# Attention sums read back packed by head and divided as rows of features, instead of turned on TensorE, divided and turned back

## The chip, the cores and the metric

One core of a Trainium2 chip runs the kernel. The metric is the device time of one execution in microseconds (us). Engines are named as in the profile: PE is TensorE (PEld its weight loads), DVE is VectorE, ACT is ScalarE, POOL is GpSimd, and SP is the engine that issues most of the DMAs.

## The reference

Two graph layers over N = 4096 nodes with 128 features. The first is masked attention with 8 heads of 16, a projection with a residual, and a feed-forward part; the second is a softmax over neighbours and a last layer norm.

```python
# layer 0
q, k, v = (layer_norm(x, g1, be1) @ w_qkv).reshape(n, 3, 8, 16) parts
scores = jnp.where(adj != 0, einsum('nhd,mhd->hnm', q, k) * SCALE, -inf)
attn = softmax(scores, axis=-1)
out = einsum('hnm,mhd->nhd', attn, v).reshape(n, 128)
x = x + out @ w_proj + b_proj
x = x + gelu(layer_norm(x, g2, be2) @ w1 + b1) @ w2 + b2
# layer 1
h = x @ Wt.T + bt
s = leaky_relu(h @ Wa.T + ba)
w = softmax(where(adj > 0, s, NEG), axis=1)
out = layer_norm_affine(x + (w @ h) @ Wp.T + bp)
```

## The kernel before

The queries are cut into 8 chunks of CH = 512, each of four subtiles of 128. The main loop goes over 512 steps (chunk, key tile of 128, half of the heads). A step makes scores on PE, masks and exponentiates them on DVE, ACT and POOL, and adds `products` to a PSUM bank. A column of ones stands behind each head's values, so each head gives 17 rows: 16 weighted sums and the denominator. The four heads of a half start at partitions 0, 32, 64 and 96. `copy_acc` (L1412) copies the finished rows of a chunk to `acc_sb`, and SP stores them in the DRAM tensor `a_dram` of shape (8, 128, 2, 512).

Then comes the tail, which the change touches, again by chunks `c`. In the kernel before a chunk goes through these steps:

- `load_sums` on SP (L247, L248): one DMA for the sums of a chunk, one for its rows of x, into two buffers by turns. Both count on the semaphore `acc_in`.
- `turn_acc` on PE (L689): eight 128x128 transposes of the sums to query-major form, into two PSUM banks.
- `normalise_att` on DVE (L484, L491): the reciprocal of the denominators, 128x32, and two products of 128x256 into `att`.
- `turn_att` on PE (L698): four transposes back to feature-major; `turned_att` on ACT (L378) copies them to `attT`.
- `project` on PE (L710): `attT` times `w_proj`.
- `first_sum` on DVE (L503 to L515): plus x and bias (`input_bias` on POOL, L318), and the layer norm's statistics; `root` on POOL (L322); `normalise_x1` on DVE (L522).
- `turn_h2` on PE (L718), `turned_h2` on ACT (L384), `ff1` on PE (L736, two instructions of the profile for one matmul of 512 columns) and `gelu` on ACT (L391), four each; `ff2` on PE (L745).
- `second_sum` on DVE (L532), `turn_x2` on PE (L728), `turned_x2` on ACT (L398), `hidden` on PE (L753) and DVE (L540), `hidden_high` (L402) and `hidden_middle` (L407) on ACT, `hidden_parts` (L546, L549) and `hidden_low` (L555) on DVE.

After that the neighbour sums of layer 1 run over all chunks (L803, L814 and others), on edges that SP began to load (`load_edges`, L255) during this stage.

There is no planner: each engine has one program in a fixed order, and semaphores order the engines against one another. An engine waits in place, so all that stands behind a waiting instruction in its program waits too. DVE's order in the tail is

```python
            for i in range(NC):
                if i >= 2:
                    hidden_low(i - 2)
                if i + 1 < NC:
                    first_sum(i + 1)
                    normalise_x1(i + 1)
                second_sum(i)
                if i + 2 < NC:
                    normalise_att(i + 2)
                if i >= 1:
                    hidden(i - 1)
                    hidden_parts(i - 1)
```

The last four steps of `products` of the main loop are woven into the start of PE's tail.

Of the kernel before, what the change touches and what calls it, by code (L numbers as in the profile page):

```python
# [8 lines left out]
ALU = mybir.AluOpType  # L9
ACT = mybir.ActivationFunctionType  # L10
# [3 lines left out]
P = 128  # L14
D = 128
H, HD = 8, 16
HG = H // 2
CH = 512
SUB = CH // P
VW = HD + 1  # L20
RT = 32
# [16 lines left out]
def gnn_kernel(nc, x, adj, adj_t, wq_rows, wk_rows, wv, w_proj, b_proj, w1, b1, w2, b2, g1, be1, g2, be2,  # L38
               Wt, wt_t, bt, Wa, ba, wp2, bp, gamma, beta, out):
    N = x.shape[0]  # L40
    NT, NC = N // P, N // CH
    TLS = 2 * NC * NT
# [5 lines left out]
    a_dram = nc.dram_tensor("attn_t", (NC, P, 2, CH), F32).ap()  # L48
# [3 lines left out]
    with ExitStack() as ctx:  # L52
        def sb(name, shape, dt):
            return ctx.enter_context(nc.sbuf_tensor(name, shape, dt))

        def sem(name):
            return ctx.enter_context(nc.semaphore(name))
# [11 lines left out]
        identf = sb("identf", [P, P], F32)  # L69
# [9 lines left out]
        ps = ctx.enter_context(nc.psum_tensor("ps", [P, 8, CH], F32))  # L79
# [73 lines left out]
        premasked = sem("premasked")  # L153
        opened = sem("opened")
# [8 lines left out]
        eb = taker(adj_words, q_words)  # L163
# [9 lines left out]

        x2_sb = wb(NT, D)
        h3 = wb(NT * 96).bitcast(BF16).rearrange("p (t k) -> p t k", k=3 * HID)
        acc, xr, xb = [eb(2, CH), eb(2, CH)], [eb(SUB, D), eb(SUB, D)], [eb(SUB, D), eb(SUB, D)]
        att, attT, x1 = eb(SUB * H, HD), eb(CH), eb(SUB, D)
        x1b, h2, h2T = eb(SUB, D), eb(SUB, D), eb(CH)
        ff, hsum, onesf = wb(FF // P, CH), eb(SUB, HID), eb(P)
        bn2, mv2, rl, rstd2 = eb(SUB, 6), eb(SUB, 2), eb(2 * SUB * HG), eb(SUB)  # L180
        x2, x2T = wb(SUB, D), wb(CH)
        hid, rest_h = wb(SUB, HID + 1), wb(SUB, HID)
        s_row, e1, e0, mx = wb(NT), wb(NT), wb(NT), wb(NT)
# [4 lines left out]
        den, aw, ew = wb(SUB), wb(SUB), wb(SUB)  # L188
# [6 lines left out]
        B_FF, B_OUT, B_ACC, B_TURN, B_HID, B_PROJ = 0, 2, 3, 5, 6, 7  # L195
# [3 lines left out]
        tail_in = sem("tail_in")  # L199
        acc_in = [sem("acc_in0"), sem("acc_in1")]  # L200
        wa_made, wa_copied, bt_step = sem("wa_made"), sem("wa_copied"), sem("bt_step")
        acc_turned = sem("acc_turned")
        rl_made, att_made = sem("rl_made"), sem("att_made")
        att_turned, attT_made = sem("att_turned"), sem("attT_made")
        projected = sem("projected")
        xb_made = sem("xb_made")
        x1_made, bn2_made, mv2_made = sem("x1_made"), sem("bn2_made"), sem("mv2_made")
# [2 lines left out]
        h2_made, h2_turned, h2T_made = sem("h2_made"), sem("h2_turned"), sem("h2T_made")  # L210
# [29 lines left out]
        def proj_bank(c):  # L240
            return B_PROJ if c > 0 else B_FF + 1

        def load_sums(sp, c):
            if c >= 2:
                sp.wait_ge(acc_turned, c - 1)
                sp.wait_ge(xb_made, c - 1)
            sp.dma_start(acc[c % 2][:, :, :], a_dram[c, :, :, :]).then_inc(acc_in[c % 2], 16)  # L247
            sp.dma_start(xr[c % 2][:, :, :], x[c * CH:(c + 1) * CH, :].rearrange("(s p) d -> p s d", p=P))\  # L248
                .then_inc(acc_in[c % 2], 16)

# [59 lines left out]
        def tail_gpsimd(pool, R):  # L310
# [1 line left out]
            pool.wait_ge(scored, TLS * R)  # L312

            def input_bias(c):
                pool.wait_ge(acc_in[c % 2], 32 * (c // 2) + 32)
                if c >= 2:
                    pool.wait_ge(x1_made, c - 1)
                nc.gpsimd.tensor_tensor(xb[c % 2], xr[c % 2], per_row(bproj_r), ALU.add).then_inc(xb_made, 1)  # L318
# [51 lines left out]
        def tail_scalar(act, R):  # L370
            act.wait_ge(tail_in, N_TAIL_IN)
            nc.scalar.activation(small[:, 7, 0:1], cols[:, 9:10], ACT.Gelu_apprx_tanh).then_inc(warmed, 1)

            def turned_att(c):
                act.wait_ge(att_turned, c + 1)
                if c >= 1:
                    act.wait_ge(projected, c)
                nc.scalar.activation(attT, ps[:, B_TURN, :], ACT.Copy).then_inc(attT_made, 1)  # L378

            def turned_h2(c):  # L380
                act.wait_ge(h2_turned, c + 1)
                if c >= 1:
# [27 lines left out]
            turned_att(0)  # L410
            act.wait_ge(wa_made, 1)
            nc.scalar.activation(wt_aug[:, HID:HID + 1], ps[:, B_HID, 0:1], ACT.Copy).then_inc(wa_copied, 1)
            turned_h2(0)
            for i in range(NC):
                gelu(i, 0)
                gelu(i, 1)
                if i >= 2:
                    hidden_middle(i - 2)
                if i + 1 < NC:
                    turned_att(i + 1)  # L420
# [48 lines left out]
        def tail_vector(dve, R, copy_acc):  # L469
# [6 lines left out]
            nc.vector.tensor_tensor(bt_r[:, HID:HID + 1], bt_r[:, HID:HID + 1], ba_r, ALU.add).then_inc(bt_step, 1)  # L476

            def normalise_att(c):
                t = ps[:, B_ACC:B_ACC + 2, :].rearrange("p g (s h k) -> p g s h k", s=SUB, h=HG)
                r = rl.rearrange("p (g s h) -> p g s h", g=2, s=SUB)  # L480
                dve.wait_ge(acc_turned, c + 1)
                if c >= 1:
                    dve.wait_ge(att_made, c)
                nc.vector.reciprocal(rl.rearrange("p (a h) -> p a h", h=HG),  # L484
                                     t[:, :, :, :, HD].rearrange("p g s h -> p (g s) h")).then_inc(rl_made, 1)
                dve.wait_ge(rl_made, c + 1)
                if c >= 1:
                    dve.wait_ge(att_turned, c)
                a = att.rearrange("p (s g h) d -> p s g h d", s=SUB, g=2)
                for g in range(2):  # L490
                    last = nc.vector.tensor_tensor(  # L491
                        a[:, :, g, :, :], t[:, g, :, :, 0:HD],
                        r[:, g, :, :].rearrange("p s (h a) -> p s h a", a=1).to_broadcast([P, SUB, HG, HD]),
                        ALU.mult)
                last.then_inc(att_made, 1)

            def first_sum(c):
                dve.wait_ge(projected, c + 1)
# [178 lines left out]
        def tail_tensor(pe, R, products):  # L677
            pe.wait_ge(tail_in, N_TAIL_IN)

            def turn_acc(c):  # L680
                pe.wait_ge(acc_in[c % 2], 32 * (c // 2) + 32)
                if c >= 1:
                    pe.wait_ge(att_made, c)
                else:
                    pe.wait_ge(opened, TLS * R)
                    pe.wait_ge(premasked, 2 * TLS * R)
                for g in range(2):
                    for s in range(SUB):
                        last = nc.tensor.transpose(ps[:, B_ACC + g, s * P:(s + 1) * P],  # L689
                                                   acc[c % 2][:, g, s * P:(s + 1) * P], identf[:, :])  # L690
                last.then_inc(acc_turned, 1)

            def turn_att(c):
                pe.wait_ge(att_made, c + 1)
                if c >= 1:
                    pe.wait_ge(h2T_made, c)
                for s in range(SUB):
                    last = nc.tensor.transpose(ps[:, B_TURN, s * P:(s + 1) * P],  # L698
                                               att[:, s * H:(s + 1) * H, :].rearrange("p h d -> p (h d)"),
                                               identf[:, :])  # L700
                last.then_inc(att_turned, 1)

            def project(c):
                pe.wait_ge(attT_made, c + 1)
                if c >= 1:
                    pe.wait_ge(x1_made, c)
                if c == 1:
                    pe.wait_ge(acc_copied[1], NC * R)
                for s in range(SUB):
                    last = nc.tensor.matmul(ps[:, proj_bank(c), s * D:(s + 1) * D], attT[:, s * P:(s + 1) * P],  # L710
                                            wp_sb, start=True, stop=True)
                last.then_inc(projected, 1)

            def turn_h2(c):
                pe.wait_ge(h2_made, c + 1)
                pe.wait_ge(attT_made, c + 1)
# [33 lines left out]
            def hidden(c):  # L750
# [4 lines left out]
                last.then_inc(hid_done, 1)  # L755

            products(TLS * R - 4)
            turn_acc(0)
            products(TLS * R - 3)
            products(TLS * R - 2)  # L760
            turn_att(0)
            products(TLS * R - 1)
            project(0)
            pe.wait_ge(acc_copied[0], NC * R)
            nc.tensor.matmul(ps[:, B_HID, 0:1], wt_raw[0:HID, :], wa_c[0:HID, :], start=True, stop=True)\
                .then_inc(wa_made, 1)
            turn_acc(1)
            turn_h2(0)
            for i in range(NC):
                ff1(i, (0, 1))  # L770
                if i + 1 < NC:
                    turn_att(i + 1)
                ff1(i, (2, 3))
                if i + 1 < NC:
                    project(i + 1)
                if i >= 1:
                    turn_x2(i - 1)
                ff2(i)
                if i + 2 < NC:
                    turn_acc(i + 2)  # L780
                if i + 1 < NC:
                    turn_h2(i + 1)
                if i >= 1:
                    hidden(i - 1)
# [890 lines left out]
```

## Time and profile before

| what | value |
|---|---|
| median of 3 runs | 1275.12 us (1273.43 to 1275.62) |
| the profiled execution | 1274.08 us |
| its span | 1272.3 us |
| mean granted clock of PE | 0.981 |
| PE busy | 1182.1 us, 93% |
| DVE busy | 1125.2 us, 88% |
| ACT busy | 1057.7 us, 83% |
| POOL busy | 957.6 us, 75% |

The shares are means over stages. The main loop takes about the first 1048 us, the tail with the feed-forward part about 100 us, and the neighbour sums the remaining 120. A stage has to be read from its own stretch, by the windows, the chain of waits and the timeline.

### The profile page before, as it was taken

The numbers are of one execution on the slowest core, as the hardware profiler recorded it, in microseconds if no ns is written. First come the engines' busy times: TensorE is split into PE (matmuls) and PEld (weight loads), VectorE is DVE, ScalarE is ACT, GpSimd is POOL, SyncE is SP. The second block draws the span as 40 slices with busy tenths as digits, with TensorE's granted clock in tenths as the row PEclk, the third lists the DMA queues.
The fourth block names the chain that finished last, engine by engine and source line by source line (L and its number), as shares of the span: only waits on it lengthen the run. The fifth ranks groups of instructions, "written<-read, shape, count | busy, mean of one in ns | idle before, by whom it ended". The sixth has DMA issues, their size and how long they took to land.

```text
span 1272.3 us, 31576 instructions
## 1 busy us (share of the span) xinstructions
PE 1182.1 (93%) x11691; PEld 337.9 (27%) x11703; DVE 1125.2 (88%) x1616; ACT 1057.7 (83%) x1202; POOL 957.6 (75%) x1012
## 2 busy tenths in 40 slices
PE   5888889999999999999999899999999998999996
PEld 2222222111111111111111111111111125775453
DVE  6989889999999999999999899999999994663655
ACT  4878889999999999999999899999999993442000
POOL 6767768999999989999998788888888873540000
PEclk8989899999999999999999999999999998999998
DMA  5332233754554455555544545554554447515881
GB/s 175 103 106 81 78 92 125 204 165 134 166 151 134 133 167 154 162 151 156 144 133 150 150 140 153 158 167 140 144 167 133 148 121 297 189 43 215 322 332 28
DMA packets 52672, 194.42 MB, mean 153 GB/s; under 512 B 6496, under 2 KB 20640, under 8 KB 42272
## 3 DMA queue, kind: packets, MB, share of 16 engines
q1 hardware_dynamic: 38944, 156.65, 34.8%
q0 software_dynamic: 9216, 33.56, 13.0%
q10 hardware_dynamic: 4352, 2.10, 0.6%
q8 instruction: 98, 1.61, 0.5%
q14 instruction: 62, 0.51, 0.1%
HBM read 114.69 MB, written 44.04 MB: 125 GB/s over the span
## 4 chain that ended last, share of the span: by engine, by line
ACT 53%; PE 25%; issue 11%; DVE 5%; POOL 5%; DMA 1%; DVEq 0%; POOLq 0%; SPq 0%
ACT probs L1299 30%; ACT probs L1293 21%; PE ps L814 4%; PE ps L1594 4%; POOL probs L1196 3%; PE ps L1609 3%; DVE probs L1402 3%; PE ps L736 2%; PE ps L803 2%; PE ps L745 2%; PE ps L1503 1%; POOL m L1189 1%; ACT kq L1274 1%; DVE acc_sb L1383 1%; PE ps L836 1%
## 5 line engine op out<-in xcount | busy, mean ns | idle before, releaser
L1402 DVE SCALAR_TENSOR_TENSOR probs<-m,ps 128x512 f32<-128x512 bf16 (+1 forms) x1024 | 926.7, 950 | 29.9 <-PE ps L1594 13.7
L1299 ACT ACTIVATE probs<-probs 128x1536 f32<-128x1536 f32 x512 | 847.3, 1656 | 0.9
L1196 POOL TENSOR_TENSOR probs<-probs,m 128x512 f32<-128x512 f32 x512 | 639.1, 1282 | 116.5 <-ACT probs L1293 106.4
L1609 PE MATMUL ps<-probs,v_sb 128*17 128x512 f32 x4096 | 543.4, 603 | 0.0
L1594 PE MATMUL ps<-kq 32*128 32x512 bf16 x6144 | 428.6, 381 | 62.2 <-DVE probs L1402 33.9
L1293 ACT ACTIVATE probs<-ps 128x512 f32<-128x512 f32 x512 | 391.6, 765 | 32.8 <-PE ps L1594 31.7
L1594 PEld LDWEIGHTS ps<-kq 32*128 32x128 bf16 x6144 | 116.6, 93 | 580.6 <-ACT probs L1293 430.1
L1189 POOL TENSOR_SCALAR m<-adj_in 128x512 bf16<-128x512 int32 x256 | 196.0, 766 | 0.2
L1609 PEld LDWEIGHTS ps<-probs,v_sb 128*17 128x17 f32 x4096 | 68.2, 95 | 219.8 <-issue 208.4
L367 POOL TENSOR_TENSOR v_sb<-v_sb,cols 128x4 f32<-128x4 f32 (+1 forms) x9 | 8.7, 968 | 98.2 <-DVE v_sb L645 98.2
L442 ACT ACTIVATE probs<-ps 128x512 f32<-128x512 f32 x8 | 4.8, 598 | 72.0 <-PE ps L791 72.0
L814 PE MATMUL ps<-kq,probs 128*128 128x512 bf16 x244 | 57.9, 386 | 0.8 <-issue 0.2
L1178 POOL DMA_DIRECT2D counts<-m x56 | 51.3, 916 | 0.1
L1162 POOL TENSOR_TENSOR q_shift<-q_shift 128x512 f32<-128x512 f32 x28 | 37.8, 1350 | 0.0
L1158 POOL TENSOR_TENSOR q_shift<-kq 128x512 f32<-128x512 bf16 x28 | 37.0, 1321 | 0.0
L384 ACT ACTIVATE q_shift<-ps,tail_words 128x512 f32<-128x512 f32 x8 | 6.2, 777 | 36.3 <-PE ps L718 36.3
L322 POOL TENSOR_TENSOR q_shift<-q_shift,cols 128x4 f32<-128x4 f32 x8 | 8.2, 1022 | 37.3 <-DVE q_shift L515 37.3
L736 PE MATMUL ps<-q_shift,tail_words 128*128 128x512 f32 x64 | 32.6, 634 | 1.9 <-ACT q_shift L384 1.7
L1390 DVE SCALAR_TENSOR_TENSOR kq<-kq,cols,tail_words 128x512 bf16<-128x512 bf16 x16 | 33.2, 2079 | 0.0
L814 PEld LDWEIGHTS ps<-kq,probs 128*128 128x128 bf16 x256 | 25.5, 102 | 28.2 <-issue 2.7
L803 PE MATMUL ps<-kq,probs 128*64 128x512 bf16 x256 | 30.7, 382 | 0.0
L745 PE MATMUL ps<-tail_words,probs 128*128 128x128 f32 x256 | 30.1, 276 | 0.3 <-ACT probs L391 0.3
(143 smaller groups left out, 620.9 us busy)
## 6 DMA issues: line engine op xcount, KB each, us to landing
adj_in<-in_adj_t SPq DMA_DIRECT2D x64, 1024.0 KB, 5.8
mask_t<-m SPq DMA_DIRECT2D x64, 512.0 KB, 2.9
counts<-m POOLq DMA_DIRECT2D x64, 512.0 KB, 4.6
kq<-mask_t SPq DMA_DIRECT2D x16, 2048.0 KB, 9.1
counts_t<-counts SPq DMA_DIRECT2D x8, 512.0 KB, 7.6
attn_t<-acc_sb SPq DMA_DIRECT2D x16, 256.0 KB, 6.5
adj_in<-attn_t SPq DMA_DIRECT2D x8, 512.0 KB, 3.9
q_shift<-in_x SPq DMA_DIRECT2D x8, 256.0 KB, 5.9
```

Of the source, the lines that this page charges most:

```text
L736: nc.tensor.matmul(ps[:, B_FF + m % 2, :], w1_sb[:, m * P:(m + 1) * P], h2T, start=True, stop=True).then_inc(ff1_done, 1)
L745: last = nc.tensor.matmul(ps[:, B_OUT, s * D:(s + 1) * D], ff[:, m, s * P:(s + 1) * P], w2_sb[:, m, :], start=m == 0, stop=m == NM - 1)
L803: last = nc.tensor.matmul(ps[r:r + HID, BANK_B[j % 2], :], h3[:, t, 2 * HID:3 * HID], edges[:, i % ERING, t % HALF, :], start=t < 2, stop= ...
L814: last = nc.tensor.matmul(ps[:, BANK_A[j % 2], :], h3[:, t, 0:2 * HID], edges[:, i % ERING, t % HALF, :], start=t == 0, stop=t == NT - 1)
L1178: copy = pool.dma_start(counts[:, :, :], m01[:, at:at + MGROUP, :], accum_op=ALU.add)
L1189: nc.gpsimd.tensor_scalar(m01[:, X % MRING, :], adj_in[:, G % 2, X % MGROUP, :], 1.0, 0.0, ALU.min, ALU.max).then_inc(mask_made, 1)
L1196: nc.gpsimd.tensor_tensor(pr, pr, m01[:, (k // 2) % MRING, :], ALU.mult).then_inc(postmasked, 1)
L1293: nc.scalar.activation(probs[:, k % SLOTS, 0, 0:CH], ps[:, bank(k, 0), :], ACT.Exp, scale=UNIT)\
L1299: nc.scalar.activation(pr, pr, ACT.Exp, scale=UNIT).then_inc(exped, 1)
L1402: nc.vector.scalar_tensor_tensor(out=pr, in0=m.to_broadcast([P, n, CH]), scalar=1.0, in1=ps[:, b:b + n, :], op0=ALU.subtract, op1=ALU.add)\
L1594: last = nc.tensor.matmul(ps[:, bank(k, hh), :], k_pack[rows(hh), g, i % 2, keys], q_pack[rows(hh), g, i, queries], start=i == 0 and not s ...
L1609: last = nc.tensor.matmul(ps[RT * hh:RT * hh + VW, 6 + g, :], v_sb[:, t, h * VW:(h + 1) * VW], probs[:, k % SLOTS, hh // 2, (hh % 2) * CH: ...
```

## The change

The sums are no longer turned. `load_sums` reads them back from DRAM already packed: for each half of the heads, one DMA brings the 4 x 16 rows of sums to 64 partitions, head behind head, and a second brings the four rows of denominators to the same 64 partitions, each repeated 16 times. That is four DMAs of 64 rows of 2 KB in place of one of 128 rows of 4 KB, and `acc_in` counts five DMAs per chunk. `normalise_att` takes the reciprocal of the repeated denominators, 128x512, and multiplies it with the sums, 128x512, straight into `attT`. `turn_acc`, `turn_att` and `turned_att` are gone. On PE `project(0)` now comes ahead of the last `products`, and `project(i + 1)` stands between the halves of `ff1(i)` instead of behind them.

```diff
-            sp.dma_start(acc[c % 2][:, :, :], a_dram[c, :, :, :]).then_inc(acc_in[c % 2], 16)
+            for g in range(2):
+                half = slice(g * HG * HD, (g + 1) * HG * HD)
+                sums = a_dram[c, :, g, :].rearrange("(h r) n -> h r n", r=RT)
+                sp.dma_start(outs[c % 2][half, 0, :], sums[:, 0:HD, :]).then_inc(acc_in[c % 2], 16)
+                sp.dma_start(outs[c % 2][half, 1, :], sums[:, HD:VW, :].to_broadcast([HG, HD, CH]))\
+                    .then_inc(acc_in[c % 2], 16)
...
-            def turned_att(c):
-                act.wait_ge(att_turned, c + 1)
-                if c >= 1:
-                    act.wait_ge(projected, c)
-                nc.scalar.activation(attT, ps[:, B_TURN, :], ACT.Copy).then_inc(attT_made, 1)
...
             def normalise_att(c):
-                nc.vector.reciprocal(rl.rearrange("p (a h) -> p a h", h=HG),
-                                     t[:, :, :, :, HD].rearrange("p g s h -> p (g s) h")).then_inc(rl_made, 1)
...
+                num, den = outs[c % 2][:, 0, :], outs[c % 2][:, 1, :]
+                dve.wait_ge(acc_in[c % 2], LOADED * (c // 2 + 1))
+                nc.vector.reciprocal(den, den).then_inc(inverted, 1)
+                dve.wait_ge(inverted, c + 1)
                 if c >= 1:
+                    dve.wait_ge(projected, c)
+                nc.vector.tensor_tensor(attT, num, den, ALU.mult).then_inc(attT_made, 1)
...
             products(TLS * R - 4)
-            turn_acc(0)
             products(TLS * R - 3)
             products(TLS * R - 2)
-            turn_att(0)
+            project(0)
             products(TLS * R - 1)
-            project(0)
...
             for i in range(NC):
                 ff1(i, (0, 1))
                 if i + 1 < NC:
-                    turn_att(i + 1)
+                    project(i + 1)
                 ff1(i, (2, 3))
-                if i + 1 < NC:
-                    project(i + 1)
                 if i >= 1:
                     turn_x2(i - 1)
                 ff2(i)
-                if i + 2 < NC:
-                    turn_acc(i + 2)
                 if i + 1 < NC:
                     turn_h2(i + 1)
```

## Rows read from the trace of the kernel before

**Rows 1.** Windows, whole core: busy us (x instructions) by engine, granted clock, DMA.

```profile
core 0: us, PE busy (x) PEld busy (x) DVE busy (x) ACT busy (x) POOL busy (x), PEclk, DMA share, GB/s
...
1060.00:1062.00 2.00, 1.13 (x3) 0.50 (x2) 0.15 (x1) 0.78 (x1) 0.51 (x1) 0.50 0.93 366
...
1090.00:1120.00 30.00, 29.92 (x212) 24.97 (x211) 21.13 (x64) 12.34 (x22) 14.61 (x13) 1.00 0.51 179
...
1138.00:1140.00 2.00, 1.45 (x13) 1.26 (x13) 1.63 (x5) 0.00 (x0) 0.34 (x1) 1.00 0.00 0
...
1180.00:1210.00 30.00, 29.84 (x192) 14.87 (x194) 16.69 (x70) 2.39 (x4) 2.08 (x2) 0.99 0.88 334
```

**Rows 2.** The chain in order of time over one chunk: start us, us, what.

```profile
1105.34 0.87 PE ps L689 x8
...
1109.50 0.44 PE ps L698 x4
...
1111.65 0.89 PE ps L710 x8
...
1112.98 3.57 PE ps L745 x32
1116.56 0.87 PE ps L689 x8
```

**Rows 3.** Timeline of DVE, one chunk: start us, us, instruction, [idle before, releaser].

```profile
1101.36 0.69 DVE L503 TENSOR_TENSOR q_shift<-ps,adj_in 128x512 f32<-128x512 f32 x1 [1.15 <-PE ps L710]
...
1105.74 0.68 DVE L532 TENSOR_TENSOR probs<-ps,q_shift 128x512 f32<-128x512 f32 x1
1106.35 0.35 DVE L484 RECIPROCAL q_shift<-ps 128x32 f32<-128x32 f32 x1
1106.73 0.76 DVE L491 TENSOR_TENSOR q_shift<-ps,q_shift 128x256 f32<-128x256 f32 x2
1107.52 0.43 DVE L540 TENSOR_TENSOR probs<-ps,tail_words 128x260 f32<-128x260 f32 x1
...
1108.96 0.41 DVE L549 TENSOR_TENSOR probs<-probs 128x256 f32<-128x256 f32 x1
1110.56 0.87 DVE L555 TENSOR_TENSOR probs<-probs 128x256 bf16<-128x256 f32 x1 [1.19 <-ACT probs L407]
```

**Rows 4.** Timeline of ACT over the same chunk.

```profile
1108.68 0.69 ACT L391 ACTIVATE probs<-ps,tail_words 128x512 f32<-128x512 f32 x1 [0.27 <-PE ps L736]
...
1110.12 0.41 ACT L407 ACTIVATE probs<-probs 128x256 bf16<-128x256 f32 x1
...
1110.90 1.47 ACT L391 ACTIVATE probs<-ps,tail_words 128x512 f32<-128x512 f32 x2
```

**Rows 5.** Groups by line, DVE, tail: busy us, mean ns, idle before.

```profile
L484 DVE RECIPROCAL q_shift<-ps 128x32 f32<-128x32 f32 x8 | 2.8, 348 | 0.0
...
L610 DVE RECIPROCAL v_sb<-v_sb 128x4 f32<-128x4 f32 x8 | 1.4, 178 | 0.3
...
L612 DVE TENSOR_TENSOR v_sb<-probs,v_sb 128x4 f32<-128x4 f32 x8 | 1.3, 162 | 0.3
```

**Rows 6.** The chain at the start of the stage.

```profile
1042.75 0.42 SPq L247
1043.22 5.71 DMA adj_in<-in_x
```

**Rows 7.** Timeline at the start of the stage, all engines.

```profile
1049.20 1.20 DVE L476 TENSOR_TENSOR tail_words<-tail_words 128x1 f32<-128x1 f32 x1
...
1052.43 1.05 PE L1609 MATMUL ps<-probs,v_sb 128*17 128x512 f32 x8
...
1054.61 0.69 DVE L503 TENSOR_TENSOR q_shift<-ps,adj_in 128x512 f32<-128x512 f32 x1 [0.37 <-PE ps L710]
...
1061.13 3.60 PE L736 MATMUL ps<-q_shift,tail_words 128*128 128x512 f32 x4 [0.87 <-ACT q_shift L384]
...
1067.81 0.69 DVE L503 TENSOR_TENSOR q_shift<-ps,adj_in 128x512 f32<-128x512 f32 x1 [7.66 <-PE ps L710]
```

More of the change, by code:

```diff
@@ L175, in gnn_kernel @@
         h3 = wb(NT * 96).bitcast(BF16).rearrange("p (t k) -> p t k", k=3 * HID)
-        acc, xr, xb = [eb(2, CH), eb(2, CH)], [eb(SUB, D), eb(SUB, D)], [eb(SUB, D), eb(SUB, D)]
-        att, attT, x1 = eb(SUB * H, HD), eb(CH), eb(SUB, D)
+        outs, xr, xb = [eb(2, CH), eb(2, CH)], [eb(SUB, D), eb(SUB, D)], [eb(SUB, D), eb(SUB, D)]
+        attT, x1 = eb(CH), eb(SUB, D)
         x1b, h2, h2T = eb(SUB, D), eb(SUB, D), eb(CH)
         ff, hsum, onesf = wb(FF // P, CH), eb(SUB, HID), eb(P)
-        bn2, mv2, rl, rstd2 = eb(SUB, 6), eb(SUB, 2), eb(2 * SUB * HG), eb(SUB)
+        bn2, mv2, rstd2 = eb(SUB, 6), eb(SUB, 2), eb(SUB)
         x2, x2T = wb(SUB, D), wb(CH)
@@ L201, in gnn_kernel @@
         wa_made, wa_copied, bt_step = sem("wa_made"), sem("wa_copied"), sem("bt_step")
-        acc_turned = sem("acc_turned")
-        rl_made, att_made = sem("rl_made"), sem("att_made")
-        att_turned, attT_made = sem("att_turned"), sem("attT_made")
+        inverted, attT_made = sem("inverted"), sem("attT_made")
         projected = sem("projected")
@@ L241, in proj_bank @@
             return B_PROJ if c > 0 else B_FF + 1
+        LOADED = 16 * 5
         def load_sums(sp, c):
             if c >= 2:
-                sp.wait_ge(acc_turned, c - 1)
+                sp.wait_ge(attT_made, c - 1)
                 sp.wait_ge(xb_made, c - 1)
-            sp.dma_start(acc[c % 2][:, :, :], a_dram[c, :, :, :]).then_inc(acc_in[c % 2], 16)
+            for g in range(2):
[4 more added lines that the diff above has]
+                    .then_inc(acc_in[c % 2], 16)
             sp.dma_start(xr[c % 2][:, :, :], x[c * CH:(c + 1) * CH, :].rearrange("(s p) d -> p s d", p=P))\
@@ L314, in input_bias @@
             def input_bias(c):
-                pool.wait_ge(acc_in[c % 2], 32 * (c // 2) + 32)
+                pool.wait_ge(acc_in[c % 2], LOADED * (c // 2 + 1))
                 if c >= 2:
@@ L408, in hidden_middle @@
                     .then_inc(h_mid_made, 1)
-            turned_att(0)
             act.wait_ge(wa_made, 1)
@@ L418, in tail_scalar @@
                     hidden_middle(i - 2)
-                if i + 1 < NC:
-                    turned_att(i + 1)
                 gelu(i, 2)
@@ L478, in normalise_att @@
             def normalise_att(c):
-                t = ps[:, B_ACC:B_ACC + 2, :].rearrange("p g (s h k) -> p g s h k", s=SUB, h=HG)
-                r = rl.rearrange("p (g s h) -> p g s h", g=2, s=SUB)
-                dve.wait_ge(acc_turned, c + 1)
+                num, den = outs[c % 2][:, 0, :], outs[c % 2][:, 1, :]
+                dve.wait_ge(acc_in[c % 2], LOADED * (c // 2 + 1))
+                nc.vector.reciprocal(den, den).then_inc(inverted, 1)
+                dve.wait_ge(inverted, c + 1)
                 if c >= 1:
-                    dve.wait_ge(att_made, c)
-                nc.vector.reciprocal(rl.rearrange("p (a h) -> p a h", h=HG),
-                                     t[:, :, :, :, HD].rearrange("p g s h -> p (g s) h")).then_inc(rl_made, 1)
[L486 to L495, printed above, removed]
+                    dve.wait_ge(projected, c)
+                nc.vector.tensor_tensor(attT, num, den, ALU.mult).then_inc(attT_made, 1)
             def first_sum(c):
@@ L678, in tail_tensor @@
             pe.wait_ge(tail_in, N_TAIL_IN)
[L680 to L701, printed above, removed]
             def project(c):
@@ L706, in project @@
                     pe.wait_ge(x1_made, c)
+                else:
+                    pe.wait_ge(opened, TLS * R)
+                    pe.wait_ge(premasked, 2 * TLS * R)
                 if c == 1:
@@ L715, in turn_h2 @@
                 pe.wait_ge(h2_made, c + 1)
-                pe.wait_ge(attT_made, c + 1)
+                if c >= 1:
+                    pe.wait_ge(h2T_made, c)
                 for s in range(SUB):
@@ L766, in tail_tensor @@
                 .then_inc(wa_made, 1)
-            turn_acc(1)
             turn_h2(0)
@@ L771, in tail_tensor @@
                 if i + 1 < NC:
-                    turn_att(i + 1)
+                    project(i + 1)
                 ff1(i, (2, 3))
-                if i + 1 < NC:
-                    project(i + 1)
                 if i >= 1:
```

## The prediction

> **What bounds the kernel now.** I read the busy times by stage first [rows 1]. Of a span of 1272.3 us the masked attention fills everything up to about 1048 us, the feed-forward part runs from there to about 1150, and the neighbour sums from there to the end. The change touches only the second stage. In it TensorE is busy for 29.92 of 30 us while VectorE has 21.13 of 30, ACT and GpSimd less than half, so at first sight work taken off TensorE is time gained. The chain of waits in order of time says the same [rows 2]: for each chunk it stays on PE from one turn of the sums (L689, 1105.34) to the next (1116.56), 11.22 us. So I asked how far the next engine is behind. VectorE's instructions over one such chunk [rows 3] have only two waits of note, 1.15 us for the projection and 1.19 us for ACT, beside the wait for GpSimd's root that lies inside the step from L503 to L532 and stays. VectorE is thus about 2.3 us per chunk short of being the bound. That margin is the number to keep.
>
> **What leaves TensorE.** Per chunk eight turns of the sums (L689, 0.87 us) and four of the outputs (L698, 0.44 us) [rows 2]: 1.31 us. But these and the moved projection (0.89, L710) were also cover. Between the last ff1 matmul and ff2 (L745) lay the projection and one turn of four, from 1111.65 to 1112.98, 1.33 us; now only the turn, 0.44, stands there. The last gelu takes about 0.75 us (two in 1.47) [rows 4], and ff2 waits for it, so some 0.35 us come back as a wait. TensorE alone would need 11.22 - 1.31 + 0.35 = 10.26 us per chunk. ACT loses a copy of 0.60 us, which was under TensorE's work and is worth nothing by itself.
>
> **What comes onto VectorE.** Removed per chunk are a reciprocal of 128x32 and two products of 128x256, together from 1106.35 to 1107.52, 1.17 us [rows 3]. Added are a reciprocal of 128x512 and a product of 128x512. The product: 128x512 of two f32 inputs took 0.69 in L503, and 128x256 in SBUF alone took 0.41 in L549 [rows 3]; I take 0.72 with the step to the next. The reciprocal decides the case. The trace has it at two sizes [rows 5]: 178 ns for 4 elements a partition, 348 ns for 32. That is 170 ns / 28 = 6.07 ns an element over a base of 154 ns. The base can be checked: the plain product of 4 elements took 162 ns and so carries nearly all of the 178. A plain operation grows by only about 1.1 ns an element (0.41 to 0.69 us from 256 to 512). So 512 elements: 0.154 + 512 x 0.00607 = 3.26 us. Bounds: if the 32-element row were slow only because it reads PSUM at a stride of 17 words, the operation would cost what a plain one does, 0.69 us; by rounding of the two rows it is not over 3.4. Against the low bound: the 4-element reciprocal reads packed SBUF and is still 16 ns, 4 ns an element, above the plain one. I take 3.25, and 3.28 with the step to the next.
>
> The Trainium skill, in "VectorE: DVE Perf Modes", First, the fixed hardware budget, says that the reciprocal is an iterated divide with a repeat count of 8. Read as eight cycles of the 0.96 GHz that it gives in its Specifications, my estimate from that page is 8.3 ns an element, 4.3 us, and about 7 us more over the kernel than the sum below. The two rows of this trace give 6.07 ns, and I keep to them.
>
> **The new chunk period.** I follow VectorE around one chunk from L532, the sum after ff2, with starts from [rows 3]. L532 to the reciprocal 0.61; reciprocal 3.28; product 0.72: attT is ready 4.61 us after L532 started. Then `hidden` (L540). From its start to L555 the shortest way is now the longer of two: on VectorE L540 to the end of L549 is 1.85 and ACT's L407 adds some 0.45; on ACT, which does `hidden_high` (L402), two gelus and `hidden_middle` (L407) in that order, it is 0.46 for L540 and its step, two copies of 0.41 (L407's; L402 is of the same shape) and two gelus of 0.6 to 0.7 between [rows 4], about 2.5. I take 2.45. L555 0.85. L503 to L532 4.38, with the wait for GpSimd in it. Sum: 4.61 + 2.45 + 0.85 + 4.38 = 12.3 us. Is TensorE inside that? After L532 starts it turns h2 and is ready for ff1 1.5 us later (four turns, 0.44 and some filling, and the 0.87 us that L736 waited for ACT behind them [rows 7]), both matmuls end at 3.5, the projection waits for attT until 4.65 and ends at 5.6, ff1's second half ends at 7.3, and ff2 waits for the last two gelus, which stand in ACT behind `hidden_middle` (start 6.6) and end at 8.2. ff2 ends at about 11.9, before VectorE asks at 12.3. So VectorE bounds by a little, the period is 12.3, and a chunk costs 12.3 - 11.22 = 1.1 us more, although TensorE has 1.31 less to do. The attT wait is also new: `project` stands first in TensorE's queue, and ff1's second half, ff2 and with it `second_sum` are queued behind it.
>
> **The start of the stage.** Before, the first x load landed at 1048.93 [rows 6] and VectorE was at the parameter sums (L476) until 1050.40; `first_sum(0)` began at 1054.61 [rows 7]. Now SP issues four loads of 128 KB in place of one, an issue being 0.42 us [rows 6], so x lands some 1.3 us or more later, about 1051.3 (between 1050.4, VectorE's own time, and 1053). Reciprocal and product end at 1055.3. Behind this on VectorE are both `copy_acc`, and on TensorE the projection and then, because of the new order, the last products (`products(TLS * R - 1)`), which were ahead of it before. Projection 1.1 (0.89 [rows 2] and its filling), products 1.05 [rows 7], the second copy 0.7 (128x512 from PSUM, as L503), steps 0.2: `first_sum(0)` at 1058.4, 3.8 us late. All up to ff1(0) shifts by this, to 1064.9 instead of 1061.13; ff1's first half took 3.60 us there at a granted clock of 0.50, the 1.2 GHz level, after TensorE had waited [rows 1, 7], and will again. The projection of chunk 1 now follows it directly, so `first_sum(1)` comes at about 1069.4 instead of 1067.81. But ff1's second half, the last gelu and ff2 come after it: 1.71 (from 1109.94 to 1111.65 in [rows 2]) + 0.75 + 3.6, so `second_sum(0)` starts at 1075.5, where it was 1067.81 + 4.38 = 1072.19. That is 3.3 us.
>
> **The loads.** In steady state the sums of a chunk are asked for almost two periods before use, and even the first load before took 5.71 us from issue to landing [rows 6]; the extra issues of SP and the wait of `input_bias` on the whole set have 20 us of cover. Only the first load has none.
>
> The Trainium skill, in "DMA: Bandwidth & Descriptors", Rules for kernel authors, row "Use all 16 engines", says that an access pattern whose outermost dimension is below 16 confines a DMA to as many engines; here that is 4, which speaks against these loads. No row before shows it.
>
> **Sum.** 3.3 at the start; from `second_sum(0)` to (1) VectorE has no `hidden` work yet and TensorE's order gives about 11.7 for 11.2, 0.5; five periods of +1.08, 5.4; the last chunk follows without a division and goes as before, 0. In all +9.2. Everything after waits for TensorE, which is full, so the shift passes through. Profiled execution 1274.08 + 9.2 = 1283.3; the median of the runs stands 1.04 above the profiled one: **1284.3 us**, slower by 0.7%.
>
> **Rivals.** *The division is cheap* (the other side). If the reciprocal runs at about the plain rate, TensorE stays the bound at 10.26 us: six chunks give 0.96 each, 5.8, and the start costs 0.3, so 1275.1 - 5.5 = 1269.6. For it: the full TensorE. Against it: [rows 5]. It decides below about 2.0 us for 512 elements, 3.6 ns each. Chance 0.06. *In between*: a reciprocal of 1.7 to 2.4 us, or VectorE's wait for ACT much shorter than I take it: 1273 to 1277.5, chance 0.04. *The first sums come late*: if the new loads use a quarter of the DMA engines, 512 KB move at a quarter of the rate. The stretch of the neighbour loads moved 334 GB/s [rows 1], so 6.3 us in place of 1.6, and with the counts stored just ahead the reciprocal starts near 1055: 1288. Chance 0.08; a mild form is in my own range. *The clock falls in the loop*: TensorE would now wait twice a chunk, 1 us each. At the 0.50 level its 9.9 us become some 18 and bind: seven chunks of 6, 1320 us. Against: it kept 1.00 from 1138 to 1140 us, where TensorE had work for 1.45 of 2 us [rows 1], and fell only where it had waited longer. Chance 0.02. The forecast itself has 0.80, with a range of its own from 1279.5 to 1288.5: the period is 12.0 to 12.7 (six times), the start 2 to 5 us.
>
> **Range and chances.** 1278.5 to 1290 leaves out the two cases below and the clock. This kernel's measurement tells 0.2%, 2.5 us, from no change. Faster 0.06, same 0.04, slower 0.90.
>
> **What would show it.** L484's successor: a reciprocal of 128x512 near 3.25 us. A period of about 12.3 us between starts of the ff2 sum. New waits of PE in the projection for the product on VectorE, about 1 us each, and VectorE without a wait except for GpSimd and ACT. `first_sum(0)` at 1058.4. It is wrong if the reciprocal takes under 2.2 us, or if ff1 shows 3.6 us a pair in later chunks.

## The result and the profile after

The changed kernel took 1296.68 us (median of 4 runs, 1294.06 to 1302.41) against 1274.55 for the kernel before beside it: a ratio of 1.0157, 95% interval 1.0123 to 1.0191. It is slower, as forecast, but by 1.57% and not 0.7%; 1296.7 lies above the range of 1278.5 to 1290. The profiled execution took 1294.06 us, its span is 1292.3 against 1272.3.

First the timeline of VectorE over one chunk of the changed kernel, which answers to [rows 3]. L477 is the reciprocal, L481 the product, L489 `first_sum`, L518 `second_sum`, L526 `hidden`, L541 `hidden_low`.

```profile
1106.03 0.69 DVE L518 TENSOR_TENSOR probs<-ps,q_shift 128x512 f32<-128x512 f32 x1 [1.04 <-PE ps L712]
1106.64 3.34 DVE L477 RECIPROCAL adj_in<-adj_in 128x512 f32<-128x512 f32 x1
1110.02 1.05 DVE L481 TENSOR_TENSOR q_shift<-adj_in 128x512 f32<-128x512 f32 x1
1110.99 0.42 DVE L526 TENSOR_TENSOR probs<-ps,tail_words 128x260 f32<-128x260 f32 x1
...
1113.35 0.42 DVE L541 TENSOR_TENSOR probs<-probs 128x256 bf16<-128x256 f32 x1 [0.90 <-ACT probs L406]
1113.69 0.68 DVE L489 TENSOR_TENSOR q_shift<-ps,adj_in 128x512 f32<-128x512 f32 x1
...
1119.18 0.69 DVE L518 TENSOR_TENSOR probs<-ps,q_shift 128x512 f32<-128x512 f32 x1 [1.04 <-PE ps L712]
```

The reciprocal takes 3.34 us where 3.25 was worked out. But the chunk takes 13.15 us, 1106.03 to 1119.18, and not 12.3, and VectorE still waits 1.04 us for ff2 at its end. So it is not simply busy. The chain in order of time over the same chunk, which answers to [rows 2], shows where the time goes:

```profile
1106.64 3.35 DVE adj_in L477
1110.05 0.05 issue
1110.10 0.05 DVEq L525
1110.15 0.84 issue
1110.99 0.43 DVE probs L526
1111.46 0.07 issue
1111.55 0.21 issue
1111.76 0.68 ACT probs L390
1112.44 0.14 issue
1112.58 1.97 PE ps L703 x4
1114.57 0.70 ACT probs L390
1115.31 3.85 PE ps L712 x32
1119.22 0.57 issue
1119.79 3.35 DVE adj_in L477
```

It is a ring through three engines: reciprocal and product (the product, L481, fills the three rows from 1110.05 to 1110.99), `hidden` on VectorE, ACT's copy of it (L401, in the two short `issue` rows from 1111.46), the gelus (L390), ff1's second half (L703), the last gelu, ff2 (L712), `second_sum` and the next reciprocal. ACT's timeline has the link that the forecast left out:

```profile
1106.47 0.78 ACT L383 ACTIVATE q_shift<-ps,tail_words 128x512 f32<-128x512 f32 x1 [3.88 <-PE ps L685]
1111.44 0.42 ACT L401 ACTIVATE probs<-probs 128x256 bf16<-128x256 f32 x1 [4.19 <-DVE probs L526]
1111.76 1.25 ACT L390 ACTIVATE probs<-ps,tail_words 128x512 f32<-128x512 f32 x2
```

ACT stands 4.19 us in `hidden_high` (L401) for VectorE, with the first two gelus of the next chunk queued behind it, although ff1's first half, whose results they take, was done about 1109.2.

Not all chunks are alike. `second_sum` (L518) starts at 1078.56, 1092.88, 1106.03, 1119.18, 1133.90, 1147.06, 1161.49 and 1171.36: of the six distances with a full chunk, three are 13.15 us and three 14.3 to 14.7. The eighth start closes the last chunk, which has no division behind it. Here are the windows of stretches inside the long ones, with the granted clock behind the busy times (columns as in [rows 1]):

```profile
1084.00:1088.00 4.00, 4.00 (x12) 2.02 (x11) 2.11 (x10) 0.69 (x1) 0.68 (x1) 0.57 0.29 95
1125.00:1129.00 4.00, 3.70 (x8) 1.65 (x8) 2.95 (x12) 2.16 (x5) 0.32 (x1) 0.57 0.39 106
1152.00:1156.00 4.00, 3.84 (x11) 2.44 (x12) 2.75 (x9) 2.18 (x5) 0.68 (x1) 0.60 0.02 4
```

There the granted clock was 0.57 to 0.60, so mostly at the lower level of 1.2 GHz, and ff1's second half took 3.52 us (chain, from 1125.73) in place of 1.97. PE's timeline shows what it did before that fall: it stood.

```profile
1120.45 1.98 PE L703 MATMUL ps<-q_shift,tail_words 128*128 128x512 f32 x4
1124.28 1.16 PE L676 MATMUL ps<-tail_words,q_shift 128*128 128x128 f32 x8 [1.84 <-DVE q_shift L481]
1125.73 3.51 PE L703 MATMUL ps<-q_shift,tail_words 128*128 128x512 f32 x4 [0.30 <-ACT probs L390]
```

The start is late too. From the timelines of SP and of VectorE there, which answer to [rows 6, 7]; first SP's, with the first issue of the sums and that of the rows of x behind it:

```profile
1042.00 0.65 SPq L250 DMA_DIRECT2D adj_in<-attn_t  x1
...
1044.39 1.29 SPq L253 DMA_DIRECT2D adj_in<-in_x  x1
```

and VectorE's:

```profile
1048.45 0.16 DVE L472 TENSOR_TENSOR tail_words<-tail_words 128x1 f32<-128x1 f32 x1
1052.60 3.35 DVE L477 RECIPROCAL adj_in<-adj_in 128x512 f32<-128x512 f32 x1 [3.99 <-DMA adj_in<-in_x]
...
1061.32 0.68 DVE L489 TENSOR_TENSOR q_shift<-ps,adj_in 128x512 f32<-128x512 f32 x1
```

VectorE waits 3.99 us for the load. `first_sum(0)` comes 6.7 us later than before, and `second_sum(0)` at 1078.56 instead of 1072.19. The account of the 20.0 us of span: start 6.4, the six distances 82.9 us in place of 67.2, 15.7; the last chunk 9.9 for 10.3; the third stage (from the last `second_sum` to the end) 120.9 for 122.6.

### The profile page after: what moved, and what is told of

The parts are those of the page before. It is cut to its first block, busy times and chain, and to the rows that moved or that the text cites. A ratio compares the mean times of both kernels' runs of the same rounds, so it can differ in the third digit from the quotient of the medians.

```text
span 1292.3 us, 31375 instructions
## 1 busy us (share of the span) xinstructions
PE 1180.4 (91%) x11607; PEld 330.2 (26%) x11607; DVE 1143.3 (88%) x1608; ACT 1052.1 (81%) x1194; POOL 955.1 (74%) x1012
## 4 chain that ended last, share of the span: by engine, by line
ACT 46%; PE 22%; issue 13%; POOL 9%; DVE 7%; DMA 2%; SPq 0%; DVEq 0%; POOLq 0%; ACTq 0%
ACT probs L1259 26%; ACT probs L1253 18%; POOL probs L1156 6%; PE ps L774 4%; PE ps L1554 4%; PE ps L1569 3%; DVE probs L1362 3%; PE ps L712 2%; PE ps L763 2%; PE ps L703 2%; DVE adj_in L477 2%; POOL m L1149 2%; PE ps L1463 1%; ACT kq L1234 1%; DVE acc_sb L1372 1%
## 5 line engine op out<-in xcount | busy, mean ns | idle before, releaser
L703 PE MATMUL ps<-q_shift,tail_words 128*128 128x512 f32 x64 | 37.2, 711 | 3.1 <-ACT q_shift L383 1.7
L390 ACT ACTIVATE probs<-ps,tail_words 128x512 f32<-128x512 f32 x32 | 21.3, 683 | 16.9 <-PE ps L703 16.8
L340 POOL TENSOR_TENSOR probs<-probs,tail_words 128x512 f32<-128x512 f32 x8 | 10.2, 1270 | 33.3 <-DVE probs L518 33.3
L712 PE MATMUL ps<-tail_words,probs 128*128 128x128 f32 x256 | 30.7, 278 | 3.2 <-ACT probs L390 3.2
```

The lines of the kernel that those rows point to most:

```text
L703: nc.tensor.matmul(ps[:, B_FF + m % 2, :], w1_sb[:, m * P:(m + 1) * P], h2T, start=True, stop=True).then_inc(ff1_done, 1)
L712: last = nc.tensor.matmul(ps[:, B_OUT, s * D:(s + 1) * D], ff[:, m, s * P:(s + 1) * P], w2_sb[:, m, :], start=m == 0, stop=m == NM - 1)
```

## The experiments

The quoted text of each is the one recorded before its run. The ratio is against the kernel before, run beside it. Runs of one kernel spread widely (the kernel before took from 1274.04 to 1283.79 us beside e1 to e4), so the times alone separate e2, e3, e4, e5 and e9 little from each other and from the changed kernel; what is said of them rests on the profiles.

**e1, the reciprocal replaced by a cheap operation.**

```diff
-                nc.vector.reciprocal(den, den).then_inc(inverted, 1)
+                nc.vector.tensor_scalar(den, den, 1.0 / 2048, None, ALU.mult).then_inc(inverted, 1)
```

> The changed kernel with the 128x512 reciprocal replaced by a product with the constant 1/2048, so the division by the denominators is left out and all loads, waits and orders stay. Theory A (the reciprocal of 3.35 us, and what is queued behind it on VectorE and, through that, on ACT and TensorE, sets the chunk period): the periods between sums after ff2 fall from 13.15 and 14.3 to 10.2 to 10.6 us, TensorE has no wait over 0.5 us in the loop, its clock stays at 1.00 there, and the time is about 1270 us, below the kernel before. Theory B (the five loads per chunk and their landing hold the stage up): the periods stay above 12.5 us and the time above 1285 us.

Measured: 1284.96 us, ratio 1.0068 (1.0040 to 1.0097). Distances of 10.5, 10.9, 14.7, 13.3, 10.8 and 10.8 us. The reciprocal is worth over 2 us a chunk, but the time is 15 us over what theory A said, and B is not right as a whole either: two chunks and the start wait for loads. In the third chunk TensorE also stood 2.29 us, and its projection and ff1's second half then took 2.08 and 2.63 us, so part of its 14.7 us is the clock. VectorE, in this chunk:

```profile
1099.49 0.69 DVE L518 TENSOR_TENSOR probs<-ps,q_shift 128x512 f32<-128x512 f32 x1 [0.83 <-PE ps L712]
1102.88 0.43 DVE L477 TENSOR_SCALAR adj_in<-adj_in 128x512 f32<-128x512 f32 x1 [2.70 <-DMA adj_in<-in_x]
```

In the changed kernel no chunk after the start waits for a load: the slow ring hid this. Both theories were half right, so the loads had to be tried by themselves.

**e2, the same loads with 16 entries in their outer dimension.** Rows go feature by feature, the heads within; `w_proj` is loaded in the same order.

```diff
-                sums = a_dram[c, :, g, :].rearrange("(h r) n -> h r n", r=RT)
-                sp.dma_start(outs[c % 2][half, 0, :], sums[:, 0:HD, :]).then_inc(acc_in[c % 2], 16)
-                sp.dma_start(outs[c % 2][half, 1, :], sums[:, HD:VW, :].to_broadcast([HG, HD, CH]))\
+                sums = a_dram[c, :, g, :].rearrange("(h r) n -> r h n", r=RT)
+                sp.dma_start(outs[c % 2][half, 0, :], sums[0:HD, :, :]).then_inc(acc_in[c % 2], 16)
+                sp.dma_start(outs[c % 2][half, 1, :], sums[HD:VW, :, :].to_broadcast([HD, HG, CH]))\
```

> The changed kernel with the rows loaded feature by feature and head by head within it, so that the outer dimension of each load has 16 entries in place of 4; the rows of w_proj are loaded in the same order, so the result is the same. Theory A (the first load is slow because its pattern keeps it on a quarter of the DMA engines): GB/s between 1044 and 1050 us rises from about 110 to above 250, the first reciprocal starts at 1049.5 to 1050.5 instead of 1052.6, and the time falls by 2 to 3 us; periods in the loop stay as they are. Theory B (the lateness comes of SP's five issues and rows of 2 KB): the first reciprocal stays at 1052 or later and the time does not change.

Measured: 1293.18 us, ratio 1.0115 (1.0064 to 1.0165). Windows from 1044 to 1050 us, the changed kernel first, then e2 (the last two columns are the busy share of the DMA engines and GB/s):

```profile
1044.00:1050.00 6.00, 5.37 (x52) 1.14 (x52) 4.46 (x8) 5.98 (x7) 2.69 (x3) 1.00 0.36 111
```

```profile
1044.00:1050.00 6.00, 5.95 (x64) 1.35 (x64) 5.49 (x9) 6.00 (x6) 3.58 (x4) 1.00 0.84 249
```

VectorE's timeline in e2, at the first reciprocal:

```profile
1049.22 0.16 DVE L474 TENSOR_TENSOR tail_words<-tail_words 128x1 f32<-128x1 f32 x1
1049.74 3.35 DVE L479 RECIPROCAL adj_in<-adj_in 128x512 f32<-128x512 f32 x1 [0.37 <-DMA adj_in<-in_x]
```

The sums come as the same bytes by the same number of issues, and the wait falls from 3.99 to 0.37 us; the median falls by 3.5. Theory A holds, B is out. The distances stayed (14.3, 13.2, 13.2, 14.7, 13.2, 13.2). That each load used just four engines is not shown by a row; the busy share of 0.36 (which has the x loads in it) fits it.

**e3, TensorE's wait filled with work that nobody uses.**

```diff
                 ff1(i, (0, 1))
                 if i + 1 < NC:
+                    for s in range(3 * SUB):
+                        nc.tensor.transpose(ps[:, 3, s % SUB * P:(s % SUB + 1) * P], identf[:, :], identf[:, :])
                     project(i + 1)
```

> The changed kernel with twelve turns of the identity matrix into an unused PSUM bank between the first half of ff1 and the projection, where TensorE now waits 1.84 us for the product on VectorE; they take about 1.3 us and nobody uses them. Theory A (the granted clock falls in some chunks because TensorE waits there): the clock stays at 1.00 from 1080 us to the end of the stage, all periods are 13.1 to 13.3 us, and the time falls by 4 to 5 us although there is more work. Theory B (the clock follows something else): periods of 14.3 us and more remain, and the time is the same or longer.

Measured: 1294.53 us, ratio 1.0122 (1.0071 to 1.0174). Windows from 1077 us to the end of the stage, of the changed kernel and of e3:

```profile
1077.00:1171.00 94.00, 78.32 (x445) 55.84 (x444) 59.62 (x127) 31.30 (x54) 35.16 (x32) 0.95 0.42 123
```

```profile
1077.00:1170.00 93.00, 84.02 (x537) 64.42 (x537) 61.57 (x137) 32.15 (x56) 36.32 (x33) 1.00 0.42 127
```

The clock stays at 1.00, the first distance is 12.65 us and the others 13.17 (1081.90 to 1160.42 is 78.5 us for six, 82.9 before). So the 14.3 to 14.7 came of the clock, and the clock of the wait: theory A on that point. The other runs bear it out: with the wait left in, the clock fell in two chunks of e2, one of e4 and three of e5, and with the turns in none, here and in e9. The time fell by 2 us, not 4 to 5, since `second_sum(0)` came 3.3 us later, at 1081.90. The first reciprocal started 2.0 us later in this execution; the other 1.3 us are the price of the edit itself, because in chunk 0 TensorE had no wait to fill and the projection began behind the turns, at 1074.47 in place of 1073.16.

**e4, ACT's copy behind the gelus.** `hidden_high(i - 2)` goes behind `gelu(i, 1)`, in place of `hidden_high(i - 1)` ahead of `gelu(i + 1, 0)`.

```diff
                 if i >= 2:
+                    hidden_high(i - 2)
                     hidden_middle(i - 2)
                 gelu(i, 2)
...
-                if i >= 1:
-                    hidden_high(i - 1)
+            hidden_high(NC - 2)
```

> The changed kernel with ACT's hidden_high of a chunk moved behind the first two gelus of the next, so that the gelus no longer stand behind a copy that waits for VectorE's sum behind the reciprocal. Theory A (the period is 13.15 and not 12.3 because gelu 0 and 1, and by their PSUM banks ff1's second half, wait for that copy): the undisturbed period falls to 12.2 to 12.5 us and the time by 4 to 6 us. Theory B (VectorE's own work sets the period): 13.15 us stays, or the period grows because VectorE now waits for the copy.

Measured: 1292.63 us, ratio 1.0115 (1.0067 to 1.0163). The undisturbed distance is 12.63 us (1080.55, 1093.18, 1105.82), one is 14.3 at the lower clock. So the copy cost 0.5 us a chunk. The first chunk of e3, where there is no copy yet, says the same: 12.65 us against 13.17. The ring through reciprocal, product, projection, ff1's second half, last gelu and ff2 is still closed, at 12.63 and not the 12.2 to 12.5 expected, and VectorE still waits at its end:

```profile
1105.82 0.69 DVE L518 TENSOR_TENSOR probs<-ps,q_shift 128x512 f32<-128x512 f32 x1 [0.92 <-PE ps L712]
```

The median is 4.0 us under the changed kernel's, at the edge of the 4 to 6 expected, with intervals that overlap. In the profiled execution the six distances gave 5.5 us, and `second_sum(0)` came 2.0 us later, mostly because the clock at the start rose some 3 us later.

**e5, the last products ahead of the first projection.**

```diff
             products(TLS * R - 2)
-            project(0)
             products(TLS * R - 1)
+            project(0)
```

> The changed kernel with the last products of the main loop put back ahead of the projection of chunk 0. Theory A (at the start the products stand behind the projection, which waits for the first reciprocal, and the copy of the last sums and the first sum wait for them): first_sum(0) starts about 2.4 us earlier against the first reciprocal, 6.3 us after its start instead of 8.7, and the time falls by 2 to 3 us. Theory B (the first load alone makes the start late): no change.

Measured: 1295.58 us, ratio 1.0139 (1.0104 to 1.0174). `first_sum(0)` started 6.24 us after the reciprocal (1058.76 and 1052.52) in place of 8.72, as expected, but `second_sum(0)` at 1078.38, where it was 1078.56. What took most of the gain is on GpSimd:

```profile
1061.62 1.26 POOL L323 TENSOR_TENSOR adj_in<-adj_in,tail_words 128x512 f32<-128x512 f32 x1 [7.31 <-DMA adj_in<-in_x]
1062.84 1.04 POOL L327 TENSOR_TENSOR q_shift<-q_shift,cols 128x4 f32<-128x4 f32 x1
```

`input_bias(1)` (L323) waits for the second set of loads, and `root(0)` (L327), for which VectorE waits 2.94 us, is queued behind it. Of the 2.6 us, 0.8 are left after that, and 0.6 more went in ff1 and the projection of chunk 1, 3.78 and 1.36 us in place of 3.46 and 1.05, since the clock rose later. So theory A was right on the start of `first_sum(0)` and wrong on the time: the product order costs almost nothing as long as the loads are late.

**e6, e1 and e2 together** (no division again).

> Both edits of the first two experiments: no reciprocal (a product with 1/2048, so the division is left out) and loads with an outer dimension of 16. Theory A (with the reciprocal away the loads became the bound in two chunks and at the start): no wait for a load after the start, all periods 10.2 to 10.9 us, first product at 1050, and the time is 8 to 11 us under that of the cheap division alone, 1273 to 1277 us. Theory B (the waits for loads came of SP's five issues a chunk or of the edge loads in front of them): periods of 13 to 15 us remain and the time is over 1280 us.

Measured: 1272.40 us, ratio 0.9973 (0.9945 to 1.0002). Distances 10.5, then five of 10.8 us; no wait for a load in the loop. Against the changed kernel's 1296.7: the loads alone gave 3.5 us, the reciprocal alone 11.7, both 24.3. They overlap in time, so neither shows its price while the other stays. Theory A: the distances are in its band, the time 0.6 us below it.

**e7, divided before repeating.** The reciprocals are taken on packed denominators, 128x32 a chunk, in the main loop (the last chunk's in the tail), stored, and read back repeated. The loads are those of e2, the order that of e5; the tail keeps the product only.

```diff
+        def invert(dve, d):
+            dve.wait_ge(dens_in, 32 * (d + 1))
+            nc.vector.reciprocal(den_sb[:, :], den_sb[:, :]).then_inc(inverted, 1)
...
             for k in range(TLS):
                 masks(k, 0)
+                if k >= 2 * NT and k % (2 * NT) == 40:
+                    invert(dve, k // (2 * NT) - 1)
```

> A full version: the reciprocal is taken on packed denominators, 128x32 for each chunk, in the main loop (for the last chunk in the tail), stored to DRAM, and read back repeated; the tail has only the 128x512 product. Loads with an outer dimension of 16, last products ahead of the first projection, projection between the halves of ff1 as in the changed kernel. Theory A (the change as made loses by reciprocal, loads, order and clock, and taking turns off TensorE is worth having by itself): periods of 10.3 to 10.8 us, clock 1.00 in the loop, time 1267 to 1272 us, faster than the kernel before. Theory B (the memory round trip or the seven reciprocals and extra DMAs in the main loop cost as much as they save): the main loop ends later than 1049 us or the time is 1274 us or more.

Measured: 1270.84 us, ratio 0.9943 (0.9915 to 0.9971): faster than the kernel before, by 0.6%, as theory A said. All distances are 10.51 us. One chunk of TensorE:

```profile
1093.87 1.98 PE L732 MATMUL ps<-q_shift,tail_words 128*128 128x512 f32 x4
1095.69 1.05 PE L705 MATMUL ps<-tail_words,q_shift 128*128 128x128 f32 x8
1096.58 1.88 PE L732 MATMUL ps<-q_shift,tail_words 128*128 128x512 f32 x4
1098.30 0.60 PE L724 MATMUL ps<-identf,probs 128*128 128x128 f32 x4
1099.24 3.84 PE L741 MATMUL ps<-tail_words,probs 128*128 128x128 f32 x32 [0.34 <-ACT probs L419]
1102.91 0.60 PE L714 MATMUL ps<-identf,q_shift 128*128 128x128 f32 x4
```

It has no wait but the 0.34 us for the last gelu, the "some 0.35 us" of the forecast. TensorE is the bound again.

**e8, the projection behind both halves of ff1**, otherwise e7.

> As the version before, but the projection of the next chunk stands behind both halves of ff1, where the kernel before had it, so that it covers the last gelu. Theory A (ff2 otherwise waits for the last gelu): 0.3 us less per period on TensorE, 9.9 to 10.4 us, and 1 to 3 us less in all if VectorE does not bind first. Theory B (VectorE binds, since its first sum now starts later): the periods are the same or longer, 10.5 to 11 us.

Measured: 1271.06 us, ratio 0.9954 (0.9928 to 0.9979). The distances are 10.92 us, longer, and VectorE's first sum now waits 1.20 us for the projection: theory B for the distance. The time is that of e7 within the intervals. The profiled execution is one of the two longest of ten, at 1279.50 us; its third stage alone took 129.9.

**e9, the reciprocal kept, with e2, e3 and e4 together.**

> The changed kernel with its reciprocal kept, and the loads' outer dimension of 16, ACT's copy moved behind the gelus, and the twelve turns that fill TensorE's wait. Theory A (reciprocal, loads, ACT's order and clock are the whole of the loss, and they add): the first reciprocal starts within 0.5 us of the end of VectorE's parameter sums, every period is 12.5 to 12.8 us at a clock of 1.00, and the time is 1283 to 1286 us, about what was predicted for the change. Theory B (something else holds it, or the turns now delay the projection): periods of 13 us or more, 1288 us or more.

Measured: 1288.50 us, ratio 1.0106 (1.0075 to 1.0137). Six distances of 12.64 us, the clock 1.00 from 1072 to 1170 us, the first reciprocal 0.47 us late: theory A on all three. The time is 2.5 us above the band expected and in that of theory B, so the four causes are not the whole of it, or do not add in full. The last chunk took 10.27 us where the changed kernel had 9.87 (in e4, with the same order on ACT, it also took 10.27), the third stage took 122.6 where it had 120.9, and at the start the turns cost 1.3 us as in e3.

**e10, e7 with the order of e4.**

> The version that divides before repeating, with ACT's hidden_high moved behind the first two gelus as in the fourth experiment. Theory A (a little of the period is still gelus behind that copy): 10.51 falls to 10.2 to 10.4 us and the time by 0.5 to 2 us. Theory B (the projection, ff1, the last gelu and ff2 on TensorE set it, the copy is hidden): 10.5 us stays.

Measured: 1268.32 us, ratio 0.9947 (0.9924 to 0.9969), not to be told from e7. The distance is 10.70 us (the first 10.52), not shorter: with the reciprocal gone the copy behind the gelus holds up VectorE instead, which waits 1.93 us for it, and the last two gelus stand behind what VectorE makes then. Theory A fell, and the 10.5 us of B was not met either.

## Why the prediction was right and wrong

The sign, and the reason for it, were right. **"What leaves TensorE"**: 1.31 us of turns go and 0.34 come back; TensorE alone needs 10.51 us (e7) where 10.26 was worked out. **"What comes onto VectorE"**: the reciprocal took 3.35 us against 3.25 from two rows at 4 and 32 elements; the line of 6.07 ns an element held over a factor of 16 to within 3%, while the Trainium skill's repeat count of 8 ("VectorE: DVE Perf Modes", First, the fixed hardware budget), read as cycles an element, gave an estimate of 4.3, which the trace does not bear out. The division is the largest cause: with the loads repaired in both, the kernel without it took 1272.40 us (e6) and with it 1293.18 (e2). With the other three causes repaired and the division left (e9) the change is still slower by 1.1%, so the sign was not luck.

Wrong was the size, in three steps: the start of the stage, TensorE's path in the new chunk period, and the clock.

**"The loads"** and **"The start of the stage"**. The start was to cost 3.3 us and cost 6.4. The first reciprocal began at 1052.60 instead of 1051.3, near the upper bound of 1053 in the text, although the main loop ended 0.7 us earlier than before; e2 takes the wait away. The late-loads rival had it right in kind; the Trainium skill's row on outer dimensions below 16 ("DMA: Bandwidth & Descriptors", Rules for kernel authors) agrees with e2, where only the order of dimensions in the loads was changed. The second part is PE's: projection and last products took 2.08 and 1.91 us, not 1.1 and 1.05: TensorE had stood 7.32 us ahead of them, and its granted clock was 0.50, the 1.2 GHz level, from 1057 to 1060 us. And "only the first load has no cover" held only while the ring was slow (e1).

**"The new chunk period"**. It said 12.3 us with VectorE as the bound, and is 13.15 with VectorE waiting 1.04 us for ff2. VectorE's own round is thus 12.1 us, nearly as worked out; what failed is "ff2 ends at about 11.9, before VectorE asks". When TensorE was followed, ff1's second half was let start at 5.6 us, right behind the projection. It takes the two PSUM banks that the first two gelus empty, and in the program `hidden_high(i - 1)` stands ahead of both gelus and waits for VectorE; when ACT was followed this order was used. In the trace ff1's second half starts 6.55 us after `second_sum` (1112.58 less 1106.03). That wait is 0.5 us of the period, by e4. Without it the ring is still TensorE's, 12.63 us in place of 11.9: reciprocal and product end 0.45 us later than was taken, projection and ff1's second half take 0.25 more, ff2 0.17 more, and the last gelus 0.14 less. Most of this is the product, 1.05 us where 0.72 was taken. In the first two chunks it took 0.69; its usual place now is beside GpSimd's `input_bias`:

```profile
1109.26 1.26 POOL L323 TENSOR_TENSOR adj_in<-adj_in,tail_words 128x512 f32<-128x512 f32 x1
```

This ends at 1110.52, and the product, begun at 1110.02, ends 0.55 us later. It does so whatever its own start: it took 1.64 us where it began 0.41 us after GpSimd's operation (e1, at 1103.34) and 1.39 where it began 0.42 us after it (e2, at 1053.13), and in all 47 products that began inside such an operation, in seven of the profiled executions, it ended 0.54 to 0.56 us after that operation. Where nothing of the kind ran beside it, it took 0.69. In e7 it began 0.16 us ahead, took 0.68, and GpSimd's operation took 1.65. So whichever of the two is second waits for the first; that they share a way to SBUF is the likely reason, and no run moved one of them alone.

**"The clock falls in the loop"** had a chance of 0.02. It did fall, in three of six chunks, and e3 shows that the waits do it; the forecast's own sign of being wrong, ff1 at 3.6 us a pair in later chunks, came with 3.44, 3.52 and 3.23. The rival as written was wrong in size: not all chunks and 6 us each, but 1.3 to 1.7 us in half of them, 4.5 together (82.93 less 12.65 for the first, as in e3, and 5 x 13.15). The argument against it was a stretch of 2 us with work for 1.45; the wait was forecast at 1 us and is 1.84 in each chunk, where the kernel before stood 0.87 us in its first and at most 0.55 in the others. Why it falls in one chunk and not in the next of the same shape stays open. The changed kernel's runs spread over 8 us, but so do those of the kernel before, so that is not shown to come of it.

The account against the forecast 9.2: the start 3.1 more; the first distance 12.65 for 11.7, 0.9; five of 13.15 for 12.3, 4.3; the clock 4.5; the last chunk 0.4 and the third stage 1.7 less. That is 19.9, the span's 20.0. The median stands 2.6 us above the profiled execution, where 1.0 was taken. With loads, ACT's order and clock repaired (e9) the kernel took 1288.5 us, still 4 above the forecast figure: its start cost 4.7 us and not 3.3, partly by the added turns, and its six distances, 12.64 us each, 8.7 and not 5.9, by the ring of e4.

## What to carry to other kernels

Before work is moved off the busiest engine, walk the ring that the moved work closes: every in-order queue it passes, and what stands in each behind a wait for it. A cheap operation on a short operand can be the dearest when the operand is first repeated; do such an operation on the packed data, early, and repeat the result. When two causes overlap, taking away one shows little, so try both together before one is acquitted.

## What the runs showed that was not expected

- VectorE's f32 reciprocal grows by 6.1 to 6.2 ns an element a partition: 178 ns at 4, 348 at 32, 3345 at 512, against 690 for a product of 512.
- The order of dimensions of a load alone, four against sixteen outer entries for the same rows, changed the rate at the start from 111 to 249 GB/s.
- Twelve useless turns a chunk, 1.5 us of TensorE work, kept its clock at 1.00 where it was 0.95, and shortened six chunks from 82.9 to 78.5 us. In the chunk where there was no wait to fill they cost 1.3 us.
- VectorE's product of two inputs in SBUF, 128x512, took 0.69 us by itself and 1.05 to 1.64 us where it began inside one of GpSimd's of 128x512; it then ended 0.55 us after that.
- The third stage, whose code was not changed, took from 120.5 to 124.4 us in the executions profiled (e3 and e7), and 129.9 in e8 (1277.8 less 1147.93), so a shift of the stage before comes through only to within some microseconds.
